# Routing of the first mixture-of-experts layer: logits by tokens, statistics spread over the attention, marks in three parts

## What is computed

```python
x = x + tanh(g_xattn[0]) * _L0_xattn_ref(_layernorm(x), ctx, ...)
x = x + tanh(g_ffn[0]) * _L0_ffn_ref(_layernorm(x), ...)       # the part changed
x = x + tanh(g_xattn[1]) * _L1_xattn_ref(_layernorm(x), ctx, ctx, gamma)
x = x + tanh(g_ffn[1]) * _L1_ffn_ref(_layernorm(x), ...)

# _L0_ffn_ref: 2048 tokens of 256 features, 32 experts in 8 groups, 4 experts a token
logits = flat @ gate_w.T
scores = sigmoid(logits)
topk_idx, topk_w = route_tokens(scores, bias_corr)  # best 4 of 8 groups, best 4 experts in them
pos = number of earlier tokens with the same expert; dropped from 128 on
h = relu2(xe @ up_w); ye = h @ down_w               # per expert, 128 places
shared = relu2(x @ shared_up_w.T) @ shared_down_w.T # every token, 512 hidden
```

## Time and profile before

| | us |
|---|---|
| median of 3 runs | 733.22 |
| lowest and highest | 731.4, 738.88 |
| profiled execution | 734.11 |
| its span, first to last instruction | 732.3 |

### The profile page before, as it was taken

One profiled execution on the slowest core, in us unless ns is written; L12 is line 12 of the kernel. 1 busy time (PEld: TensorE's weight loads), 2 busy tenths in 40 slices (PEclk: granted clock), 3 DMA queues, 4 the chain that ended last, 5 costly groups with the idle time before them and its releaser, 6 DMA issues.

```text
span 732.3 us, 13733 instructions
## 1 busy us (share of the span) xinstructions
PE 652.4 (89%) x4737; PEld 343.0 (47%) x4738; DVE 517.6 (71%) x1238; ACT 370.8 (51%) x616; POOL 355.1 (48%) x409
## 2 busy tenths in 40 slices
PE   3789999999999989989864778999989899999997
PEld 1233333333333336677541334445543367777754
DVE  3788989888889479946336898999873863333336
ACT  2147788788777634445330565666642203444430
POOL 3845646656431110077276886762010036777735
PEclk9999999999999999999995799999999999999999
DMA  6945545565633194044653667975317412222228
GB/s 149 211 108 137 147 124 140 151 177 148 171 95 88 46 308 82 6 150 139 192 166 96 190 202 194 231 208 157 109 40 235 118 33 70 87 89 88 68 95 282
DMA packets 110151, 101.12 MB, mean 138 GB/s; under 512 B 26344, under 2 KB 95629, under 8 KB 109611
## 3 DMA queue, kind: packets, MB, share of 16 engines
q1 hardware_dynamic: 100259, 80.52, 39.6%
q0 software_dynamic: 8352, 18.74, 9.1%
q10 hardware_dynamic: 1472, 0.99, 0.7%
HBM read 58.49 MB, written 24.40 MB: 113 GB/s over the span
## 4 chain that ended last, share of the span: by engine, by line
PE 58%; DVE 15%; issue 8%; POOL 7%; DMA 7%; SPq 3%; ACT 2%; POOLq 0%; ACTq 0%; DVEq 0%
PE O L478 12%; PE S L433 11%; PE ST L1569 6%; DVE mx L597 4%; POOL spare L305 4%; PE ST L441 3%; DMA QS<-mxT 3%; PE M L1586 2%; PE S L1586 2%; PE M L527 2%; PE M L520 2%; PE ST L1481 2%; SPq L170 1%; DMA PX<-xn,TI 1%; PE M L503 1%
## 5 line engine op out<-in xcount | busy, mean ns | idle before, releaser
L597 DVE TENSOR_REDUCE mx<-S 128x2 f32<-128x512 f32 x384 | 251.2, 684 | 37.0 <-PE S L433 35.1
L353 ACT ACTIVATE PX<-ST 128x1024 f32<-128x1024 f32 x192 | 196.1, 1023 | 95.3 <-PE ST L441 91.7
L433 PE MATMUL S<-QS 62*128 62x256 bf16 (+1 forms) x768 | 151.2, 292 | 37.0 <-DVE mx L597 29.0
L441 PE MATMUL ST<-QS 64*128 64x256 bf16 (+1 forms) x768 | 140.7, 277 | 4.5 <-DMA QS<-mxT 4.5
L478 PE MATMUL O<-PX,VA 128*32 128x256 f32 x1536 | 122.7, 392 | 0.1
L433 PEld LDWEIGHTS S<-QS 62*128 62x128 bf16 (+1 forms) x768 | 48.5, 97 | 153.9 <-DVE mx L597 98.7
L305 POOL DMA_INDIRECT spare<-ye,GI x64 | 68.2, 1066 | 26.4 <-issue 12.6
L1687 POOL DMA_INDIRECT PX<-xn,TI x39 | 39.8, 1020 | 52.6 <-DVE K1n L1881 37.2
L441 PEld LDWEIGHTS ST<-QS 64*128 64x128 bf16 (+1 forms) x768 | 53.8, 96 | 19.0 <-issue 9.0
L810 POOL DMA_INDIRECT PX<-xn,TI x32 | 34.1, 1065 | 53.6 <-DVE spare L1196 44.1
L284 POOL TENSOR_TENSOR X<-X,rd 128x256 f32<-128x256 f32 x16 | 11.6, 726 | 86.0 <-ACT rd L363 86.0
(11 more groups left out here) (299 smaller groups left out, 1119.9 us busy)
## 6 DMA issues: line engine op xcount, KB each, us to landing
QS<-QKs SPq DMA_DIRECT2D x93, 128.0 KB
QS<-keys SPq DMA_DIRECT2D x16, 512.0 KB, 5.5
keys<-spare SPq DMA_DIRECT2D x96, 64.0 KB, 2.3
QS<-QKs SPq DMA_DIRECT2D x93, 64.0 KB
EGU<-in_ew SPq DMA_DIRECT2D x16, 256.0 KB, 4.4
xn<-spare SPq DMA_DIRECT2D x8, 512.0 KB, 10.9
ye<-QKc SPq DMA_DIRECT2D x32, 128.0 KB, 2.1
VA<-in_val SPq DMA_DIRECT2D x16, 256.0 KB, 3.7
```

Source lines behind the costliest of these rows:

```text
L353: e.activation(M["PX"][pair % 4][:, :], M["ST"][pair % 2][:, :], ACT.Exp, scale=A.scale).then_inc(A.exp, 1)
L433: got = e.matmul(M["S"][n % 2][:, 256 * a:256 * a + 256], QS[:, 0, 128 * a:128 * a + 128], QS[:, 1, :], start=True, stop=True)
L441: got = e.matmul(M["ST"][(NP * t + k // 2) % 2][:, 512 * u + 256 * a:512 * u + 256 * a + 256], QS[:, 1, 128 * a:128 * a + 128], QS[:, 0, : ...
L597: e.tensor_reduce(M["mx"][b % 2][:, :, A.row_of_max(head)], M["S"][n % 2][:, :].rearrange("p (a s) -> p a s", a=2), AX.X, ALU.max, negate= ...
```

## The change

In the first feed-forward layer alone. (1) `bn_stats` of batches 0 to 10 move to steps 4 to 14, the aggregations to steps 8, 12 and 14, the normed rows of batches 0 to 7 to steps 10 and 13. (2) Transposes and column copies of batches 0 to 7 move to step 14, those of 8 to 11 to step 15. (3) The logits are made with the tokens as stationary operand: two products of 128x128 with 32 gate columns for each batch, straight into tokens by experts; `logit_rows`, their copies and the transposes back are gone. Those of groups 0 and 1 stand in step 15, of group 2 in step 16. (4) Hidden chunks 0 to 3 go into steps 16 and 17, between the last pieces of the attention. (5) The marks come in three parts: batches 0 to 7 in step 16, 8 to 11 and 12 to 15 behind the pipeline. (6) RR is made by ScalarE and GpSimd, and the table waits for both. (7) `down` of batches 10 and 11 moves behind the experts, between hidden chunks 13 and 14, and the third `shared_added` into step 0 of the second attention.

```diff
 def ffn0_pool(e, w, G, M):
+    w.wait_ge(G.dve, G.at["R"])
...
+    e.tensor_tensor(of_batch(M["RR"][:, :, 1, :]), of_batch(M["R"]), batch, ALU.mult).then_inc(G.rr, 1)
...
+    def logits(g):
         w.wait_ge(G.xt, 2 * g + 2)
-        w.wait_ge(G.lc, g)
...
+        w.wait_ge(G.sig, g - 1)
+        for n in range(GB * g, GB * g + GB):
+            for a in range(2):
+                got = e.matmul(BK[1][:, E0 * n:E0 * n + E0], XT[:, a, 128 * n:128 * n + 128], M["GW"][:, a, :],
+                               start=(a == 0), stop=(a == 1))
         got.then_inc(G.lg, 1)
 
     def at(t, k):
-        if t == NB - 1 and k in (2, 5, 9, 13):
-            transposed((2, 5, 9, 13).index(k))
+        if t == NB - 2 and k in (6, 9, 11, 13):
+            transposed((6, 9, 11, 13).index(k))
+        if t == NB - 1:
+            if k == 1:
+                logits(0)
+            if k == 5:
+                logits(1)
+            if k in (9, 13):
+                transposed(4 if k == 9 else 5)
...
+                logits(2)
+                hidden(e, w, G, M, 0)
+            if k == 6:
+                hidden(e, w, G, M, 1)
+            if k == 13:
+                hidden(e, w, G, M, 2)
+        if t == NB + 1 and k == 1:
+            hidden(e, w, G, M, 3)
...
-    hidden(e, w, G, M, 12, 13, 14, 15)
+    hidden(e, w, G, M, 12, 13)
     w.wait_ge(G.ey, E0)
-    down(e, w, G, M, 3)
+    down(e, w, G, M, 10, 11)
+    hidden(e, w, G, M, 14, 15)
+    down(e, w, G, M, 12, 13, 14, 15)
...
         w.wait_ge(G.dve, G.at["OH", q])
+        w.wait_ge(G.rr, 1)
+        w.wait_ge(G.sig, 4)
...
-        if t == NB + 1 and m == 0:
+        if t == NB - 1 and m == 7:
             sigmoids(0, 2)
...
     relu_squared(e, w, G, M, 10, 11)
-    copied_out(e, w, G, M, 8, 12)
+    w.wait_ge(G.dve, G.at["R"])
+    e.activation(M["RR"][:, :, 0, :], M["R"], ACT.Copy, scale=M["pcol"][:, 0:1]).then_inc(G.sig, 1)
+    copied_out(e, w, G, M, 8, 10)
...
+        if 4 <= t < 15 and k == 2:
+            row(t - 4)
+        if t in (8, 12) and k == 4:
+            statistics(t // 4 - 2)
+        if t in (10, 13) and k in (4, 6, 8, 12):
+            normed_rows((0 if t == 10 else 4) + (4, 6, 8, 12).index(k))
         if t == NB - 2:
             if k == 5:
                 constants()
-                statistics(0, rows(0, 4))
...
+            if k in (8, 11, 13, 15):
+                columns((8, 11, 13, 15).index(k))
...
+        if t == NB:
+            if k == 1:
+                row(12)
+                marks(10)
             if k == 14:
-                columns(3)
...
+                marks(5)
```

More of the change, by code:

```diff
@@ L892, in hidden, with down @@
         got.then_inc(G.up, 1)
-def down(e, w, G, M, g):
-    w.wait_ge(G.sq, 4 * g + 4)
-    for b in range(GB):
-        n = GB * g + b
+def down(e, w, G, M, *batches):
+    for n in batches:
+        g, b = n // GB, n % GB
+        w.wait_ge(G.sq, 4 * g + 4)
         w.wait_ge(G.xs, n - 1)
@@ L1202, in ffn0_dve_meanwhile, with row, statistics @@
     mv = M["fmv"]
-    def rows(lo, hi):
-        for b in range(lo, hi):
-            w.wait_ge(A.x, b + 1)
-            got = e.bn_stats(M["f6"][:, b, :], M["X"][:, b, :])
-        return got
-    def statistics(g, last):
-        last.then_inc(G.bn, 1)
+    def row(b):
+        w.wait_ge(A.x, b + 1)
+        got = e.bn_stats(M["f6"][:, b, :], M["X"][:, b, :])
+        if b % GB == GB - 1:
+            got.then_inc(G.bn, 1)
+    def statistics(g):
         w.wait_ge(G.bn, 3 * g + 1)
@@ L1305, in at @@
     def at(t, k):
+        if t == 0 and k == 6:
+            shared_added(e, w, G, M, 2)
         if t == 1 and k == 6:
```

158 lines of the change are left out of this document (56 added, 102 removed).

## The result

The changed kernel takes 757.55 us (median of 4 runs, 750.43 to 764.56), the kernel before 734.64 beside it on the same chip: ratio 1.0295, 95% interval [1.0246, 1.0343]. Slower, as forecast, but by 22.9 us and not by 12.5, and beyond the range given (735 to 752). The run of 764.56 stands in the median but not in the ratio, since it lies over 1.5% above the fastest; without it the median is 756.93. The profiled execution took 758.18, 24.1 more than that of the kernel before.

What follows compares the result with a forecast made beforehand. VectorE, nearly full in a steady attention step, was taken to bound up to the table, then GpSimd's gathers. Terms 3.2 + 5.0 + 5.3 - 3.3 + 2.0 + 0.3 = +12.5 on 734.11 gave 746.6, median 745.7; range 735 to 752.

Steps and rivals of the forecast that it cites:

- Term 1: Attention steps 4 to 13: spread bn_stats, aggregations and normed rows on VectorE push maxima on the chain, +3.2 us.
- Term 2: Steps 14 and 15: added transposes, two groups of logits and a stall for a column copy on TensorE, +5.0 us.
- Term 3: Last values to last bn_stats: the first marks hold back the reciprocal of batch 15, +5.3 us.
- Rival B: Marks end early enough, TensorE's order sets the start of the last bn_stats, 2.6 us earlier: 743.1 us, chance 0.15.
- Term 4: Last bn_stats to the table: VectorE's 8.8 us less work, limited by TensorE and ScalarE, -3.3 us.
- Term 5: Start of the second attention: two batches of down ahead of hidden chunks 14 and 15 delay SyncE's loads, +2.0 us.
- the addition: Third shared addition in step 0 of the second attention: 1.6 us against idle of 1.4, +0.3 us.
- Rival D: Before the table: GpSimd's product and VectorE's one-hots exclude each other, one-hots end 4.1 us later: 746.7 us, chance 0.07.
- Rival E: Table load holds ScalarE for an unseen 1.5 us too, ahead of the marks' sigmoid: 747.2 us, chance 0.05.
- the drain: ScalarE's table load: by a skill's rule each switch adds 1.38 us, total an estimated 1.4 us more.
- Rivals A and C: A: VectorE alone decides, 728.1 us, chance 0.12; C: VectorE's 7.3 us in the loop lie on the chain, 749.8, 0.14.

Runs made afterwards that it cites:

- e10: Kernel before with only the bn_stats, aggregations and normed rows spread over steps 4 to 13; ratio 1.0046 to the kernel before.
- e1: Changed kernel with the third column copy of step 14 at k=12 instead of k=13, ahead of the product that waits for TensorE; 752.02 us, ratio 1.0246.
- e6: e1 with the first marks (batches 0 to 7) put back behind the pieces of the attention; 756.37 us, ratio 1.0280.
- e3: Changed kernel with the first marks (batches 0 to 7) put back behind the pieces of the attention; median 771.21 us, fastest run 755.27.
- e13: Kernel before with logits by tokens in steps 16 and 17, four transposes earlier, the sigmoid's table load behind the last eviction; 732.81 us, ratio 0.9994.
- e7: e1 with three unread repeats of hidden chunk 0's products in TensorE's idle places; 747.18 us, ratio 1.0178.
- e14: e5 run once more, beside e15 on the same chip; 747.45 us, ratio 1.0185.
- e15: e9 run once more, beside e14 on the same chip; 745.04 us, ratio 1.0152.
- e5: e1 with both table values (RR) made by VectorE again; 746.73 us, ratio 1.0176.
- e18: e13 with ScalarE making one table value ahead of the squares of chunks 10 and 11, first marks stage behind batch 15's product; 758.44 us, ratio 0.9959.
- e8: Kernel before with the third column copy of step 15 at k=13 instead of k=10, so that TensorE waits; 735.59 us, ratio 1.0008.
- e2: Changed kernel with logits of groups 0 and 1 moved to step 16, their sigmoid behind ScalarE's last eviction, TensorE's wait kept; 754.28 us, ratio 1.0282.
- e11: e9 with the three unread repeated products of e7 in TensorE's idle places; ratio 1.0125.
- e9: e5 with the order of down, hidden chunks 12 to 15 and third shared addition around the experts undone; ratio 1.0176.

## Why the prediction was wrong in size

- **Term 1** (+3.2): right, +3.3 in the profile, +3.4 in e10. The parts are less exact than their sum: from one reciprocal at k=0 to the next, the six steps with a row alone are 0.12 longer on average (forecast 0.15), but t=8, 10, 12 and 13 are 0.63, 1.44, 0.21 and 0.36 longer where I had about 0.6 for each, so part of the hit is luck.
- **Term 2** (+5.0) is the step that failed, by 7.2 us. Its parts were nearly right at the full clock: in e1 the way from the loop's end to T0 takes 5.3 us more than before, of which 1.2 are the transposes and 3.9 the two groups, 1.94 each where I took 1.45 (16 passes at 0.12, not at the 0.09 of the transposes of 32 columns). The wait of 0.9 us I foresaw to the tenth (0.86). What I did not ask is what the wait does to the clock: I priced the clock only in the tail, where the profile showed it, and took "TensorE has no gap here" to mean that a wait costs its own length. The wait brought the clock down there, and the half clock cost 6 us more than the wait itself (6.05 between e1 and the changed kernel).
- **Term 3** (+5.3): right, +6.0; reciprocal 11.2 behind T0 (forecast 10.8), R0 17.5 (16.8). e6 shows the cause. Rival B (TensorE sets R0) was not the case, except in e3 at the half clock.
- **Term 4** (-3.3) failed by 4.1. The chain was the right one: last hidden chunk, square, ScalarE's value (1.99; forecast 1.8), table in one piece (released by L1056, as I had asked the profile to show). The term in it that was mis-sized is "I add 1.0" for the clock: it stood at 0.50 for 17 us, and the transposes, logits and chunks 4 and 5 took 5.1 us more than at full speed (1.97 against 1.03 in e13, 3.63 against 1.94, 6.09 against 3.6). That is the 4.1 by which the term failed and the 1.0 that I had added. e7 gives part of it back (2.6 of R0 to the table). I had seen that TensorE would idle 6 us and taken the price from the earlier trace rows, 2 us of a stretch that lasts 3.4 there, in a place where TensorE idles about 1.2.
- **Term 5** (+2.0, with the addition +2.3): 0.0 in the profile, 2.4 between the medians of e14 and e15 but 0.35 between their profiles, 1.7 on average over the profiles, whose ranges overlap. Neither shown nor refuted.
- **The shape of the sum** was wrong with it: I added terms, each from undisturbed rows, and gave the clock no rival and, but for 1.2 us at the high end of term 3, no end of the range. **Rival D** happened: the one-hots were stretched by 3.3 us beside GpSimd's product (5.72 us, estimated 4.1), hidden behind ScalarE's value, so that not even its +1 came. The Trainium skill, "GPSIMD Engine Reference", section "Specifications", names that contention; e5 agrees, with 9.26 against 12.56. **Rival E** did not: the table load started 0.03 behind the last exponential, took 1.28, and the sigmoid followed in 0.01, so neither the unseen part nor the drain that the prediction names beside it came. **Rivals A and C** did not happen.

## What to carry over

Before adding a wait or an instruction that can cause one to an engine stretch without gaps, look at TensorE's granted clock around every wait that is already there: a wait of 0.9 us cost 6 more here in the profile, and moving one copy by one head took them away. Where a profile shows TensorE near idle at the end of a phase, put real work there (hidden chunks, not filler) and compare distances at the same clock. Move a value to another engine only where that engine waits anyway, and not behind the last piece of work that the same consumer needs: the same ScalarE product cost 4.1 us (with GpSimd's half) in one place and cost nothing that can be seen in e18 in another.

## What the runs showed that I had not expected

- TensorE's clock fell to 0.50 within 2 us behind a single wait of 0.86 us and stayed there while the engine was busy without a gap: for 3.4 us (e8), 10 us (e2, and the changed kernel) and 41 us (e3). The wait of 0.56 at the end of the loop did not do it in any profile. A wait is not the only way: in the changed kernel the clock fell once more, for 3.4 us at 258.2, 15 us behind the last wait; why is open.
- 16 f32 passes of 32 columns, each with its own stationary operand, take 1.94 us at the full clock, 0.12 each, and 3.62 at half. The Trainium skill, "TensorE: Matmul & The Clock Gate", section "Wait — 56ns, not 53.3ns?", gives 25 ns as the smallest distance at this width; these f32 passes, with a weight load of 128 columns ahead of each, stay far above it, and no run here separates the two.
- GpSimd's product of 2048 bf16 elements takes 5.72 us and adds 3.3 to 9.26 us of VectorE's comparisons in SBUF beside it, all of it in one comparison (5.58 instead of 2.29).
- Useless matmuls made a kernel faster: by 4.8 us between the medians of e7 and e1, 3.1 of them ahead of the table in the profiles, and e11 against e9, on one chip, by 5.1 us.
